# Attention and mixture-of-experts layer on one core: two blocks of the tensor engine's transition between batches are put in another order

## The reference

```python
def layer(x):
    q, k, v = (x @ Wq.T, x @ Wk.T, x @ Wv.T)        # 32 heads of 8, q and k rotated (rope)
    kmean = mean of k over chunks of 32 tokens
    gate  = q . kmean                                # top 4 chunks a query, own chunk forced
    p     = softmax(q . k * scale, allowed chunks, causal)
    o     = p @ v
    g     = (x @ Wg1.T) @ Wg2.T                      # low rank: Wg1 is 8 x 256
    o     = rmsnorm(o) * o_norm_weight * sigmoid(g)
    x1    = layernorm(x + o @ Wo.T)
    # mixture of experts on x1: 2 shared experts, 16 routed, 4 chosen, hidden width 176
    out   = x1 + shared(x1) + sum_e gate_e * (relu(x1 @ w1_e + b1_e) @ w2_e + b2_e)
    return layernorm(x1 + out)
```

## Time and profile before

| | |
|---|---|
| median of 3 runs | 1475.87 us (1475.16 to 1476.57) |
| profiled execution | 1475.45 us, of it 1473.4 us span |
| busy share PE, DVE, ACT, POOL | 91, 74, 57, 36 % |
| mean granted clock of PE | 0.958 |
| chain that ended last | PE 49 %, DVE 25 %, ACT 12 %, issue 5 %, DVE's queue 4 % |

### The profile page before, as it was taken

The page is one execution under the profiler, slowest core; times in us unless marked ns, Lnnn a source line. Parts: engine busy times, 40 slices in busy tenths (PEclk is TensorE's granted clock), DMA queues, the critical chain, the costliest instruction groups (busy, mean ns, idle before and its releaser), DMA issues.

```text
span 1473.4 us, 29057 instructions
## 1 busy us (share of the span) xinstructions
PE 1342.5 (91%) x10992; PEld 738.3 (50%) x10992; DVE 1092.0 (74%) x2747; ACT 840.4 (57%) x1266; POOL 532.7 (36%) x638
## 2 busy tenths in 40 slices
PE   5687999999998999989999999989999899999697
PEld 3322475436654366535654366543764347553364
DVE  6993688857897588966888578975789668885534
ACT  5406773396635875287733966358762777439221
POOL 3203542254323542245422543235422454225143
PEclk8757999999999999999999999999999999999799
DMA  6001032200221011210222002210212102220031
GB/s 240 16 14 16 15 87 67 52 18 21 95 66 37 30 61 62 67 31 16 86 67 52 19 21 93 68 35 30 59 59 70 32 16 67 72 51 16 16 112 60
DMA packets 52283, 77.81 MB, mean 53 GB/s; under 512 B 6334, under 2 KB 26800, under 8 KB 51888
## 3 DMA queue, kind: packets, MB, share of 16 engines
q1 hardware_dynamic: 52144, 75.96, 17.5%
HBM read 67.02 MB, written 8.65 MB: 51 GB/s over the span
## 4 chain that ended last, share of the span: by engine, by line
PE 49%; DVE 25%; ACT 12%; issue 5%; DVEq 4%; POOL 3%; DMA 2%; SPq 0%; POOLq 0%
PE PS L569 10%; PE PS L557 9%; PE PS L713 7%; ACT UQ L987 7%; DVE CM L1351 6%; DVE hr L1158 4%; PE PS L487 4%; PE PS L504 3%; POOL hp L1046 3%; ACT UK L987 2%; DVEq L1150 2%; PE PS L768 2%; PE PS L408 2%; PE PS L723 2%; DVE CM L1270 2%
## 5 line engine op out<-in xcount | busy, mean ns | idle before, releaser
L1046 POOL TENSOR_TENSOR hp<-hr,hp 128x512 f16<-128x512 f32 (+1 forms) x200 | 236.8, 1184 | 606.8 <-ACT hp L844 542.8
L1351 DVE TENSOR_REDUCE CM<-PS 128x32 f32<-128x1024 f32 x320 | 378.7, 1219 | 40.0 <-PE PS L487 36.0
L569 PE MATMUL PS<-W,hp 128*128 128x256 f16 (+1 forms) x2400 | 314.6, 274 | 18.7 <-POOL hp L1046 16.8
L557 PE MATMUL PS<-x1T,W 128*128 128x512 f16 (+1 forms) x1200 | 311.9, 387 | 0.0
L569 PEld LDWEIGHTS PS<-W,hp 128*128 128x128 f16 (+1 forms) x2400 | 214.3, 98 | 106.7 <-POOL hp L1046 44.2
L835 ACT ACTIVATE hr<-PS,CF 128x512 f32<-128x512 f32 (+1 forms) x200 | 136.9, 685 | 194.3 <-PE PS L557 189.1
L844 ACT ACTIVATE hp<-hr 128x512 f16<-128x512 f32 (+1 forms) x178 | 112.5, 632 | 232.8 <-DVE hr L1158 219.8
L1158 DVE TENSOR_TENSOR hr<-hr,gB 128x512 f32<-128x512 f32 x176 | 126.2, 717 | 67.7 <-ACT hr L835 61.7
L557 PEld LDWEIGHTS PS<-x1T,W 128*128 128x128 f16 (+1 forms) x1200 | 108.5, 100 | 113.1 <-issue 35.8
L987 ACT ACTIVATE UK<-PS 128x1024 f32<-128x1024 f32 x160 | 153.2, 1040 | 11.1 <-PE PS L504 10.7
L987 ACT ACTIVATE UQ<-PS 128x1024 f32<-128x1024 f32 x160 | 150.7, 1044 | 3.0 <-PE PS L504 1.5
(11 more groups left out here) (150 smaller groups left out, 1796.4 us busy)
## 6 DMA issues: line engine op xcount, KB each, us to landing
gB<-gates SPq DMA_DIRECT2D x64, 256.0 KB, 3.3
gB<-gates SPq DMA_DIRECT2D x32, 224.0 KB, 2.9
gB<-gates SPq DMA_DIRECT2D x32, 192.0 KB, 2.9
gB<-gates SPq DMA_DIRECT2D x32, 160.0 KB, 2.6
xT<-in_xT SPq DMA_DIRECT2D x8, 512.0 KB, 5.3
qET<-rows SPq DMA_DIRECT2D x16, 256.0 KB, 5.1
v<-in_x SPq DMA_DIRECT2D x8, 512.0 KB, 4.0
gB<-gates SPq DMA_DIRECT2D x32, 128.0 KB, 2.9
```

The lines of the kernel that those rows point to most:

```text
L557: mm = pe.matmul(PS[0:w, BK_H[c % 2], :], W1[:, a, k, bass.ds(f0, w)], x1T[:, e, k, :], start=(n == 0), stop=(n == 5))
L569: mm = pe.matmul(PS[:, BK_Y + j // 2, (j % 2) * D:(j % 2 + 1) * D], hp[0:w, slot, a, j * P:(j + 1) * P], W2[0:w, e, bass.ds(c, 1), :].rear ...
L1046: nc.gpsimd.tensor_tensor(hp[0:w, slot, 1, :], hr[0:w, slot, :], hp[0:w, slot, 0, :], ALU.subtract).then_inc(pool_hp, 1)
L1351: nc.vector.tensor_reduce(dst, src, AX.X, ALU.max).then_inc(dve_cm, 1)
```

## The change

Two blocks on PE and one on ACT change places; nothing is added or removed.

```diff
@@ def turn(b, m, more):  (PE)
-                if m is not None:
-                    x1_transpose(m)
                 pe.wait_ge(dve_rope, b * NT + 2)
                 transpose_q(b, 0, 2)
+                if m is not None:
+                    x1_transpose(m)
                 pe.wait_ge(dve_rope, (b + 1) * NT)
                 transpose_q(b, 2, NT)
                 chunk_means(b)
@@
                 if m is not None:
                     for part in range(3):
                         up(m, 1, part)
+                rank_rows(b)
                 pe.wait_ge(act_v, 2 * b + 2)
                 if m is not None:
                     gate_rows(m)
-                rank_rows(b)
@@ def turn(b, m, more):  (ACT)
                 stack_high(b, 3, NT)
+                rank_copy(b)
                 if m is not None:
                     gate_rows(m)
-                rank_copy(b)
```

More of the change, by code:

```diff
@@ L575, in turn @@
             def turn(b, m, more):
+                pe.wait_ge(dve_rope, b * NT + 2)
+                transpose_q(b, 0, 2)
                 if m is not None:
                     x1_transpose(m)
-                pe.wait_ge(dve_rope, b * NT + 2)
-                transpose_q(b, 0, 2)
                 pe.wait_ge(dve_rope, (b + 1) * NT)
```

## The result

The changed kernel takes 1478.72 us (median of 12 runs, 1475.79 to 1481.39) against 1475.68 us (12 runs, 1474.2 to 1477.14): ratio 1.0022, interval 1.0013 to 1.0031. The forecast of 1476.4 us lay 2.3 us too low, inside its range (1473.7 to 1479.2) but on the edge of what it called no change. The profiled execution took 1480.39 us (span 1478.3), so it is one of the slower ones of its series.

The account below looks back on a forecast made before the run. PE, 91 % busy, was held by DVE's rotation and POOL's `low` of chunk 1, so filling waits gains little. Part 1 0, part 2 -0.8 + 1.35 = +0.55 us: 1475.87 to 1476.4 us, range 1473.7 to 1479.2 (eight in ten).

Parts of the forecast that it names:

- Part 1, "value 0": PE, four query transposes ahead of x1's: idle time moves 1.5 us later, unfilled; 0, bounds 3.2 us gained and 0 lost.
- Part 2, low-clock turn, +0.45: PE and ACT, low-rank product and copy ahead of gates' rows: `down` of chunk 1 0.45 us later in turns 2, 5, 6.
- Part 2, full-clock turn, -0.2: Same move in turns 1, 3, 4, 7: `low` of chunk 1 on POOL limits the gain to 0.2 us a turn.
- Does it carry on?: Behind `down` of chunk 1: DVE's 1.08 us wait at chunk 5 is slack above 0.2, so the gain passes.
- the sum of part 2: Low-rank product and copy moved, all turns: -0.8 us at full clock and +1.35 us at low clock, +0.55 us.
- "A delay passes anyhow": Behind `down` of chunk 1: a delay there runs on through PE and ACT to DVE; 0.45 us a low-clock turn.
- Rival C: Idle directly ahead of PE's chunk means lowers the clock in more turns, 1.45 us each, up to 1482.2 us; chance 0.09.
- Rivals A and B: A: PE's fills count in full, 1469.6 us, chance 0.04. B: no clock falls in turns 2, 5, 6, 1472.1 us, 0.05.

Follow-up runs that it names:

- two series: Only the four query transposes moved ahead of x1's, against the kernel before: 1476.61 against 1475.12 us, then 1475.98 against 1475.31 us.
- part 2 alone: Only the low-rank product moved ahead of the gates' rows on PE and its copy ahead of theirs on ACT, against before: 1477.91 us, ratio 1.0018.
- experiment 2: Kernel before with the first four query transposes done ahead of x1's and again in their old place behind: 1475.44 us, ratio 0.9997.

## Why the prediction was right in its range and wrong in its sum

- Part 1, "value 0": right by the rows, 2.01 us before and after. What it gave no price is the clock: +1.5 and +0.7 us in two series, the second not clear of noise, with no row moved.
- Part 2, low-clock turn, +0.45: measured +0.48 at `down` of chunk 1 (15.83 against 15.35) and +0.47 at the product of chunk 5. Right, and by the way that it gave: relu of chunk 1 0.56 us later, `low` 0.54.
- Part 2, full-clock turn, -0.2: at `down` of chunk 1 measured -0.32 (14.21 against 14.53), so the step is right and a little small (`low` of chunk 1 itself 0.24 earlier, 0.2 forecast, and PE's new wait for it 0.41 us, 0.5 forecast). The step that failed is "Does it carry on?". It took DVE's idle 1.08 us at chunk 5 for slack that a shift of 0.2 can't use up. That slack depended on two collisions with POOL; the shift made a third of 1.0 us. Instead of -0.2 it is +0.23. With four full-clock turns this turns the sum of part 2 from +0.55 into 4 x 0.23 + 3 x 0.47 = +2.3 us, and part 2 alone measured +2.4 at equal clock. "A delay passes anyhow", for the low-clock turns, held.
- That the measured time lies in the range is luck in this respect: the range was made wide for the number of low-clock turns, which went from three to four in the profile, and the larger part of the 2.3 us by which the forecast was too low comes from a step with the wrong sign, 4 x (0.23 + 0.2) = 1.7 us. It was also a close thing, 0.5 us below the upper end.
- Rival C (the clock falls in more turns) was given 0.09 for five of seven turns and more. The profile shows four of seven, and a second fall elsewhere in the turn in two turns, before in one. The mean clock of the 12 runs is 0.9564 (standard error 0.0007), of before 0.9578 (87 runs), worth some 0.9 us by the common slope. So a lower clock is likely a part of the loss, and it isn't the whole of it.
- Rivals A and B fell: PE was early, the kernel wasn't, and the clock went down, not up.
- The sum for one execution: before to after 4.9 us. Of this 1.05 us lie ahead of turn 1 (x1's first transpose at 182.28 against 181.23), where only the first batch's attention runs, whose order hardly changes (the two runs differ there in where the clock is low); the turns have 3.9. One more transition at the lower clock is worth about 0.8 us and one more fall elsewhere about 0.9 (turn 2 takes 172.69 us before, with one fall, and 173.56 with two in experiment 2, where the rows of the turn are those of before); that leaves some 2.2 us for 3 x 0.23 + 4 x 0.47 = 2.6. One execution of each can't settle the 1.05.

The Trainium skill (SBUF — State Buffer, section on the two separate sides) says that VectorE and GpSimd share one pair of ports, which is locked whole: whichever instruction starts first keeps it to its end and the other stands still, for VectorE instructions in a two-port mode or with two SBUF inputs (these only against a GpSimd instruction that reads SBUF, as `low` and the stacks do). With that rule the trace agrees: L1284, L1286, L1287 and L1292 have two such inputs, were held to the end of the POOL instruction that they met and ended 0.04 to 0.56 us behind it, `low` was held in its turn by a scan that had started 0.07 us earlier, and MAX8 with one input (L1270) took 0.15 us a record beside POOL and 0.16 without it. The rule stood against the forecast's full-clock step and was not weighed there; the 1.27 and 1.62 us of turn 3 were in the trace of before.

## What to carry to other kernels

A gap in the list of waits is worth filling only if the work behind it isn't held by a second engine; read what the next two or three meetings of engines wait for, and whether the slack there is made of times that would change with the shift. Where two engines hold each other, such slack is not a number: an instruction 0.2 us earlier may meet another partner and cost 1.0. Work cut into pieces to fit a gap has to be priced in pieces: three of four matmuls took as long as the four. And an order that leaves every row in its place may still change how often the clock falls; so the comparison needs many runs and their mean clocks beside the one profile.

## What the runs showed of the hardware that was not expected

- The time of a run follows its mean granted clock: 0.65 us for 0.001 within a kernel, over 205 runs of before and ten other kernels. In one series of before 1472.28 us goes with 0.962 and 1477.97 us with 0.951.
- DVE's instruction of 0.18 to 0.20 us takes 1.14 to 1.22 us beside a POOL instruction of 1.15 to 1.26, ending just behind it; and POOL's own instruction is held by DVE as well, 1.57 us against 1.15 behind a scan of 0.69 us.
- Two matmuls of 8 rows that write different rows of the result run beside each other, 0.007 us apart. Of four such matmuls three take 0.96 us, as all four do, and one alone 0.53 us.
- Doing the queries' first four transposes twice costs nothing measurable (0.9997, 0.9986 to 1.0008) where doing them once in the other place cost about 1 us in the mean of two series, one of them not clear of noise.
